# Queries of the last two attentions, projected with tokens on partitions and turned afterwards

## The reference, cut to what matters

```python
# layer 2: 16 heads of 128, 4 key/value heads; rms norm over a head, after a bias
q = (hidden_states @ Wq + bq).reshape(b, s, NH, HD).transpose(0, 2, 1, 3)
q = _rmsnorm(q, qn_w)                     # q * rsqrt(mean(q*q) + eps) * qn_w
scores = jnp.einsum('bhsd,bhed->bhse', q, k) * scale + attention_mask
# layer 3: no bias, but rotary position after the norm; keys from context and stream
q = (draft_hidden @ Wq.T).reshape(bsz, draft_len, H, HD)
q = _rms_norm(q, q_norm_w).transpose(0, 2, 1, 3)
q = _rope(q, draft_position_ids)          # x * cos(emb) + rotate_half(x) * sin(emb)
k = _rope(k, full_position_ids)
```

## Time and profile before

| | us |
|---|---|
| median of 3 runs | 1300.43 (1300.22 to 1301.52) |
| profiled execution | 1304.3 |
| its span in the trace | 1302.5 |

### The profile page before, as it was taken

One profiled execution on the slowest core, in us unless ns is written; L12 is line 12 of the kernel. 1 busy time (PEld: TensorE's weight loads), 2 busy tenths in 40 slices (PEclk: granted clock), 3 DMA queues, 4 the chain that ended last, 5 costly groups with the idle time before them and its releaser, 6 DMA issues.

```text
span 1302.5 us, 22884 instructions
## 1 busy us (share of the span) xinstructions
PE 1147.4 (88%) x8124; PEld 844.3 (65%) x8147; DVE 850.5 (65%) x1920; ACT 621.5 (48%) x1407; POOL 352.9 (27%) x328
## 2 busy tenths in 40 slices
PE   4867869999969999899999988888998999999894
PEld 3554644444455665889988746666657888898753
DVE  7788966888867663455546585333497777775664
ACT  5575435677733343344433422222266766666252
POOL 0040011222121002222222146566422433334032
PEclk8756976999969999899999889899999999999998
DMA  7010034000032235000000262522371000000100
GB/s 257 2 44 1 1 137 203 1 2 2 2 134 91 88 140 174 1 2 1 1 1 1 92 288 84 196 85 86 101 289 66 17 18 17 17 9 9 49 1 33
DMA packets 44571, 89.30 MB, mean 69 GB/s; under 512 B 7280, under 2 KB 30448, under 8 KB 42672
## 3 DMA queue, kind: packets, MB, share of 16 engines
q1 hardware_dynamic: 39184, 73.45, 15.7%
q0 software_dynamic: 5280, 14.42, 3.4%
...
## 4 chain that ended last, share of the span: by engine, by line
PE 65%; DVE 18%; issue 6%; ACT 5%; DMA 2%; POOL 2%; SPq 1%; another core or an unknown queue 1%; DVEq 0%; ACTq 0%; POOLq 0%; PEldq 0%
PE psum L2566 5%; PE psum L2154 4%; PE psum L3183 4%; PE psum L2126 4%; PE psum L3155 3%; PE psum L2586 3%; PE psum L1702 2%; PE psum L1274 2%; PE psum L3056 2%; PE psum L3103 2%; PE psum L2079 2%; PE psum L3125 2%; PE psum L3490 2%; PE psum L2057 2%; PE psum L1720 2%
## 5 line engine op out<-in xcount | busy, mean ns | idle before, releaser
L1469 DVE TENSOR_REDUCE c_max<-psum 128x2 f32<-128x512 f32 x128 | 84.2, 680 | 19.7 <-PE psum L1274 18.2
L1369 ACT ACTIVATE c_probs<-psum 128x512 f32<-128x512 f32 x128 | 75.1, 597 | 35.6 <-PE psum L1285 35.4
L2566 PE MATMUL psum<-m_experts,m_tileT 128*128 x188 | 69.2, 493 | 19.2 <-issue 13.4
L3183 PE MATMUL psum<-a_wo,a_outT 128*128 128x256 f32 x256 | 75.1, 405 | 0.7 <-DVE x_tok L3365 0.7
L2208 ACT ACTIVATE a_probs<-a_probs,a_max 128x64 f32<-128x64 f32 x128 | 42.7, 334 | 44.9 <-DVE a_max L2264 44.9
L3263 ACT ACTIVATE a_probs<-psum,a_max,a_q_rstd 128x128 f32<-128x128 f32 x128 | 56.8, 458 | 11.3 <-DVE a_max L3313 11.2
L2566 PEld LDWEIGHTS psum<-m_experts,m_tileT 128*128 128x128 f32 x188 | 35.8, 199 | 38.6 <-issue 27.9
L2126 PE MATMUL psum<-ctxT_yT_hi,a_wq 128*128 128x128 f32 x256 | 52.9, 290 | 8.2 <-DVE a_qT L2250 7.1
L2875 POOL DMA_INDIRECT m_back<-m_out_tiles,m_rows_of_slots x47 | 46.8, 995 | 46.9 <-DVE m_out_tiles L2809 39.6
L2643 ACT ACTIVATE m_tile_silu<-psum 128x176 f32<-128x176 f32 x47 | 14.9, 318 | 91.0 <-PE psum L2566 56.3
L2250 DVE TENSOR_TENSOR a_qT<-psum,a_columns 128x512 f32<-128x512 f32 x32 | 22.0, 688 | 55.4 <-PE psum L2126 55.4
...
...
## 6 DMA issues: line engine op xcount, KB each, us to landing
...
```

Of the source, the lines that this page charges most:

```text
L1369: e.activation(c1P[:, n % 8, :, :], ps[:, 2 + n % 2, :].rearrange("p (k t) -> p k t", k=2), ACT.Exp, scale=float(1.0 / np.sqrt(np.float32( ...
L1469: e.tensor_reduce(c1M[:, u % 2, j, :], ps[:, c1_score_bank(n), :].rearrange("p (q t) -> p q t", q=2), AX.X, ALU.max).then_inc(c1_mx, 1)
L2566: ins = e.matmul(ps[:, 4 + t % 2, 0:M2_UP], m2xT[:, t % 2, kc, :], m2e[:, bass.ds(own + kc * M2_UP, M2_UP)], start=(kc == 0), stop=(kc == ...
L3183: ins = e.matmul(ps[:, 7, 0:D], a3at[:, i % 2, h, :, :], a3wo[:, h, :], start=(h == 0 and g is None), stop=(h == HQ - 1), skip_group_check ...
```

## The change

- Tokens become the stationary operand and the weights the moving one: two matmuls of 512 columns per group, and the result has tokens on partitions.
- Attention 2: VectorE adds a bias row that is laid out over all partitions (a2_q_bias, 1 MB, loaded over the weights of the keys), writes a2_q_tok, ScalarE squares that, VectorE sums the squares per head (squares_reduced), TensorE turns the group into bank 5 (queries_turned) and ScalarE copies it to a_qT (queriesT). Turned keys move to bank 4, shared with the values.
- Attention 3: ScalarE squares the raw bank; VectorE multiplies by cosine and, half by half, by sine straight from PSUM (queries_read), adds (queries_rotated) and sums the squares (squares_reduced); TensorE turns the group, into the same bank as the raw queries, and ScalarE copies it. The two copies with swapped halves go.
- The square-sum matmuls go. square_sums becomes four small instructions that spread the sums over the partitions that need them, one slot earlier than before.
- In the loops queries_turned comes after heads_out in attention 3 (before keys_turned), and after keys and values in attention 2. In a3_dve queries_read comes before the maxima.
- Queries and keys now use tables of the same form, so MoE 1 makes only one set (two VectorE steps and one ScalarE step fewer, two loads and two stores fewer), and the table of the queries is fetched as the odd 64-element pieces of it, with a small row of norm weights beside. The column tables of attention 3 go.

```diff
-        TRIG_DVE_AT = {9: (0, 0), 10: (0, 1), 11: (1, 0), 12: (1, 1)}
-        TRIG_ACT_AT = {11: 0, 13: 1}
-        TRIG_OUT_AT = {10: 0, 12: 1}
+        TRIG_LOADED = 16 * 2
+        TRIG_DVE_AT = {9: 0, 10: 1}
+        TRIG_ACT_AT = 11
+        TRIG_OUT_AT = 10
...
+        a2bq = nc.alloc_sbuf_tensor_at("a2_q_bias", [P, HQ * HD], F32, offset=ARENA + 4 * KC * HK * HD)
+        m("a2_q_bias_upper", [P, HQ * HD // 2], F32)
...
+            e.wait_ge(*a2_cr.at(NT))
+            e.wait_ge(m1_st, 16 * TILES)
+            e.dma_start(a2bq[:, :], a["a2_bq"].unsqueeze(0).broadcast_to([P, HQ * HD])).then_inc(a2_in.sem, 16)
...
             def queries(g):
                 i, j = g // 4, g % 4
                 if g:
+                    e.wait_ge(*a2_qb.at(g))
+                for kk in range(KC):
+                    ins = e.matmul(ps[:, 6, :], a2tok[kk][:, 1, i * P:(i + 1) * P], a2wq[:, kk, j * 512:(j + 1) * 512], start=(kk == 0), stop=(kk == KC - 1))
+                ins.then_inc(a2_qp.sem, 1)
+
+            def queries_turned(g):
+                e.wait_ge(*a2_qb.at(g + 1))
+                if g:
                     e.wait_ge(*a2_q.at(g))
-                out = ps[:, 6, :].rearrange("p (b h t) -> p b h t", b=2, h=4)
                 for h in range(4):
-                    for kk in range(KC):
-                        ins = e.matmul(out[:, :, h, :], a2wq[:, kk, (4 * j + h) * HD:(4 * j + h + 1) * HD], a2tok[kk][:, 1, i * P:(i + 1) * P],
-                                       start=(kk == 0), stop=(kk == KC - 1))
-                ins.then_inc(a2_qp.sem, 1)
-
-            def out_and_squares(n):
-
-                u, g = a2_group(n, A2_OUT), a2_group(n, 2 - A2_AHEAD)
-                c = (n + 1) % 4
-                if c == 0 and n >= -1:
-                    e.wait_ge(*a2_sr.at(min((n + 5) // 4, NT)))
-                if g is not None:
-                    e.wait_ge(*a2_qf.at(g + 1))
-                if u is not None:
-                    i = u // 4
-                    e.wait_ge(*a2_o.at(2 * i + 1 + c // 2))
-                    if c == 0 and i:
-                        e.wait_ge(*a2_res.at(i))
-                for k in range(4):
-                    if g is not None:
-                        b2, p_ = k // 2, 2 * (g % 4) + k % 2
-                        at_ = D + (p_ // 4) * 8 + (p_ % 4) * 2 + b2
-                        s_ = b2 * 256 + (k % 2) * P
-                        ins = e.matmul(ps[:, 7, at_:at_ + 1], a2qs[:, g % 4, s_:s_ + P], onesf[:, 0:1], start=(c == 0 and k == 0), stop=True,
-                                       skip_group_check=True)
-                        if k == 3:
-                            ins.then_inc(a2_sp.sem, 1)
...
+                    ins = e.transpose(ps[:, 5, h * P:(h + 1) * P], a2qk[:, g % 2, h * HD:(h + 1) * HD], identf[:, :])
+                ins.then_inc(a2_qtp.sem, 1)
+
+            def out_projected(u):
+                i, c = u // 4, u % 4
+                e.wait_ge(*a2_o.at(2 * i + 1 + c // 2))
+                if c == 0 and i:
+                    e.wait_ge(*a2_res.at(i))
+                for h in range(4 * c, 4 * c + 4):
+                    ins = e.matmul(ps[:, 7, 0:D], a2at[:, i % 2, h, :, :], a2wo[h // 8][:, h % 8, :], start=(h == 0), stop=(h == HQ - 1))
+                if c == 3:
+                    ins.then_inc(a2_wp.sem, 1)
...
             def query_squares(g):
-                e.wait_ge(*a2_q.at(g + 1))
-                if g >= 4:
-                    e.wait_ge(*a2_sp.at(g - 3))
-                e.activation(a2qs[:, g % 4, :], a2qT[:, g // 4 % 2, g % 4, :], ACT.Square).then_inc(a2_qf.sem, 1)
+                e.wait_ge(*a2_qb.at(g + 1))
+                if g >= 2:
+                    e.wait_ge(*a2_qd.at(g - 1))
+                e.activation(a2qs[:, g % 2, :], a2qk[:, g % 2, :], ACT.Square).then_inc(a2_qf.sem, 1)
+
+            def queriesT(g):
+                i, j = g // 4, g % 4
+                e.wait_ge(*a2_qtp.at(g + 1))
+                if i >= 2:
+                    e.wait_ge(*a2_s.at(2 * (i - 2) + j // 2 + 1))
+                e.activation(a2qT[:, i % 2, j, :].rearrange("p (b h t) -> p b h t", b=2, h=4), ps[:, 5, :].rearrange("p (h b t) -> p b h t", b=2, h=4),
+                             ACT.Copy).then_inc(a2_q.sem, 1)
...
             def square_sums(i):
-                e.wait_ge(*a2_sp.at(4 * i + 4))
+                e.wait_ge(*a2_qd.at(4 * i + 4))
                 if i >= 2:
                     e.wait_ge(*a2_rq.at(i - 1))
-                e.tensor_scalar(a2qss[:, i % 2, :], ps[:, 7, D:D + 16], HD * 1e-6, None, ALU.add).then_inc(a2_sr.sem, 1)
+                for odd in range(2):
+                    for b2 in range(2):
+                        ins = e.tensor_scalar(a2qss[S * odd:S * odd + S, i % 2, b2:16:2], a2qa[S * b2:S * b2 + S, i % 2, odd:16:2], HD * 1e-6, None, ALU.add)
+                ins.then_inc(a2_sr.sem, 1)
 
             def queries(g):
+                j = g % 4
+                e.wait_ge(*a2_qp.at(g + 1))
+                if g >= 2:
+                    e.wait_ge(*a2_qf.at(g - 1))
+                    e.wait_ge(*a2_qtp.at(g - 1))
+                e.tensor_tensor(a2qk[:, g % 2, :], ps[:, 6, :], a2bq[:, j * 512:(j + 1) * 512], ALU.add).then_inc(a2_qb.sem, 1)
+
+            def squares_reduced(g):
                 i, j = g // 4, g % 4
-                v4 = "p (b h t) -> p b h t"
-                e.wait_ge(*a2_qp.at(g + 1))
+                e.wait_ge(*a2_qf.at(g + 1))
                 if i >= 2:
-                    e.wait_ge(*a2_s.at(2 * (i - 2) + j // 2 + 1))
-                bias = bc(a2c[:, 4 * j:4 * j + 4], 1, 2).unsqueeze(3).broadcast_to([P, 2, 4, S])
-                e.tensor_tensor(a2qT[:, i % 2, j, :].rearrange(v4, b=2, h=4), ps[:, 6, :].rearrange(v4, b=2, h=4), bias, ALU.add).then_inc(a2_q.sem, 1)
+                    e.wait_ge(*a2_sr.at(i - 1))
+                e.tensor_reduce(a2qa[:, i % 2, 4 * j:4 * j + 4], a2qs[:, g % 2, :].rearrange("p (h d) -> p h d", h=4), AX.X, ALU.add).then_inc(a2_qd.sem, 1)
...
-            e.dma_start(a3tr[:, :, :], a["a3_trig"][:, 1, :, :]).then_inc(a3_tq.sem, 16)
+            own = a["a3_trig"].rearrange("p x (i r t) -> p (x i) r t", r=2, t=S)[:, :, 1, :]
+            e.dma_start(a3tr[:, :, :], own).then_inc(a3_tq.sem, 16)
+            e.dma_start(a3qrow[:, :, :], a["a3_q_rows"].unsqueeze(0).broadcast_to([P, 2, HD])).then_inc(a3_tq.sem, 16)
...
-            e.tensor_scalar(a3qcs[:, 0, :], a3tr[:, 1, :], a3c[:, 0:1], None, ALU.mult)
-            dve_step(e, e.tensor_scalar(a3qcs[:, 1, :], a3tr[:, 0, :], a3c[:, 6:7], None, ALU.mult))
+            sin, cos = a3tr[:, 0:NT, :], a3tr[:, NT:2 * NT, :]
+            qc, qs = (a3qcs[:, r, :].rearrange("p (i a t) -> p i a t", i=NT, a=2) for r in range(2))
+            e.tensor_tensor(qc, bc(cos, 2, 2), bc(a3qrow[:, 0, :].rearrange("p (a t) -> p a t", a=2), 1, NT), ALU.mult)
+            e.scalar_tensor_tensor(qs[:, :, 0, :], sin, -1.0, bc(a3qrow[:, 1, 0:64], 1, NT), ALU.mult, ALU.mult)
+            dve_step(e, e.tensor_tensor(qs[:, :, 1, :], sin, bc(a3qrow[:, 1, 64:128], 1, NT), ALU.mult))
...
-                if a3_q_free(g) > 0:
-                    e.wait_ge(*a3_qr.at(a3_q_free(g)))
-                out = ps[:, a3_q_bank(g), :].rearrange("p (b h t) -> p b h t", b=2, h=4)
+                if g == A3_LEAD:
+                    e.wait_ge(*a3_qr.at(g))
+                elif g >= 2:
+                    e.wait_ge(*a3_q.at(g - 1))
+                for kk in range(KC):
+                    ins = e.matmul(ps[:, a3_q_bank(g), :], a3tok[kk][:, 1, i * P:(i + 1) * P], a3wq[:, kk, j * 512:(j + 1) * 512],
+                                   start=(kk == 0), stop=(kk == KC - 1))
+                ins.then_inc(a3_qp.sem, 1)
+
+            def queries_turned(g):
+                e.wait_ge(*a3_rot.at(g + 1))
+                e.wait_ge(*a3_qr.at(g + 1 if g < A3_LEAD - 1 else min(g + 2, A3_U)))
+                if g == A3_U - 1:
+                    e.wait_ge(*a3_q.at(g))
                 for h in range(4):
-                    for kk in range(KC):
-                        ins = e.matmul(out[:, :, h, :], a3wq[:, kk, (4 * j + h) * HD:(4 * j + h + 1) * HD], a3tok[kk][:, 1, i * P:(i + 1) * P],
-                                       start=(kk == 0), stop=(kk == KC - 1))
-                ins.then_inc(a3_qp.sem, 1)
-
...
+                    ins = e.transpose(ps[:, a3_q_bank(g), h * P:(h + 1) * P], a3rot[:, g % 2, h * HD:(h + 1) * HD], identf[:, :])
+                ins.then_inc(a3_qtp.sem, 1)
...
+                if a3_unit(n, 2 - A3_AHEAD) is not None:
+                    queries_turned(n + A3_AHEAD - 2)
...
-            def queries(g):
+            def query_squares(g):
                 e.wait_ge(*a3_qp.at(g + 1))
                 if g >= 4:
-                    e.wait_ge(*a3_sp.at(g - 3))
-                bank = a3_q_bank(g)
-                e.activation(a3qs[:, g % 4, :], ps[:, bank, :], ACT.Square)
-                if g >= 2:
-                    e.wait_ge(*a3_q.at(g - 1))
```

(62 more changed lines are left out.)

192 lines of the change are left out of this document (84 added, 108 removed).

## The result

The changed kernel takes 1333.04 us (median of four runs, 1328.47 to 1336.35) against 1300.33: a ratio of 1.025, interval 1.0218 to 1.0282. It is slower, as forecast, but by 33 us and not by 9.5, and it lies above the range (1328). The profiled execution took 1336.03, its span is 1334.2 against 1302.5.

The account below looks back on a forecast made before the run. In both attention middles only TensorE's work and its waits were taken to count. Attention 2 -7.4, attention 3's middle +7.1 and head +9.6 gave +9.3, rounded to 9.5: median 1310 us, range 1285 to 1328.

Parts of the forecast that it names:

- the price of the four square-sum instructions: Attention 3's middle: in one of two even slots they stand ahead of VectorE's read and take 0.4 to 0.8 us.
- the bound of the middle (+13): Attention 3's middle, forecast +7.1 us: slow bound, if GpSimd slows VectorE's two-input instructions or the small ones are held.
- The clock: Rival, chance 0.20: each late even slot of attention 3 drops the clock, idle past some 1.3 us; +11 to +16, 1325.
- My sign for this rival: Granted clock below 0.95 in attention 3's middle would show that late even slots drop the clock.
- The same-bank wait: Attention 3: turning waits for VectorE's read of the next group in bank 6; TensorE idles 1.1 to 1.6 us, even slots.
- TensorE's saving: TensorE's work per group of queries falls by 0.5 us per slot, nearer 0.4 where no output projection runs.
- P + 2.20: Attention 3's middle: P is a slot's first score matmul; the turning wants its bank released 2.20 us later.
- Attention 2's head: Attention 2, slots 0 to 6: the already late query bias gets 1.3 us worse in two places, +2.6.
- Slots 0 to 6 of attention 3: VectorE's lateness without output projections to cover it: slots 1 to 6 from 38.5 to 44.6 us, low-clock spells +3.
- The leading slots of attention 3: Seven slots start 1 us later for the query tables but wait less for ScalarE: +0.5 us.
- Edits costed at nothing: Query angles leaving MoE 1, the bias row's load, attention 3's sines fetched in pieces: range -0.5 to +2 us.
- The weight loads: Rival, chance 0.02: TensorE's time follows its weight loads; 16 fewer save 3 us per slot, 60 in attention 2, 1235.

Follow-up runs that it names:

- (3): Changed kernel with attention 3's four small square_sums instructions as length-one reductions instead of additions of a constant (constant left out): 1310.0 us, ratio 1.0085.
- (12): Changed kernel with GpSimd's key product in attention 3 covering only 8 of 128 columns per head from the fifth batch on: 1299.17 against 1276.02, ratio 1.0196.
- (8): Changed kernel with 28 extra, unread identity turnings ahead of queries_turned in each attention 3 slot that has the square sums: 1326.14 us, ratio 1.0185.
- (1): Kernel before, with the change made in attention 2 only: 1297.01 us, ratio 0.9978.
- (7): Changed kernel, attention 3: queries turned into bank 2, square_sums behind queries_read, leading slots project group n+7 before turning n+5, turned queries copied after keys: 1298.21 us, ratio 0.9975.
- 10: Changed kernel with attention 3's square_sums as reductions, and squares_reduced there cut to four elements per partition: 1276.53 against 1272.93, ratio 1.0026.
- (9): Changed kernel with attention 3's four square_sums additions done by ScalarE behind its squares instead of by VectorE: 1278.98 against 1272.93, ratio 1.0044.

## Why the prediction was wrong

- **The step that failed** is the price of the four square-sum instructions, "0.4 to 0.8", bounded by the duration of a reciprocal. They take 2.35 us where GpSimd works. The trace of before had a sign of it in reach: two long GpSimd instructions stand together in each even slot (1096.97 and 1097.97), and beside them VectorE's product of two operands in SBUF took 0.97 us (1098.58) and not 0.68 (1105.18, GpSimd idle). The walk through the slot never put GpSimd beside VectorE; I named the case only in the bound of the middle (+13).

```profile
L3325 DVE TENSOR_TENSOR a_q_sin<-a_q_halves_swapped,ctx_tok x18: 681/827/1005, 1043.3 to 1175.0; 128x512 f32<-128x512 f32 x18
```

- **What the hold cost**, with the low clock behind it: attention 3 takes 299.1 us with it and 275.4 without (3), 23.7 less, about the whole miss of 23. That the kernel then takes 1310.0, the very time that I gave, is luck: its leading slots cost 4.3 us and not 0.5, slots 0 to 6 cost 7.3 and not 9.1, the middle 2.0 and not 7.1, and attention 2 gives 3.3 (in the changed kernel) and not 7.4.
- **The clock**, a rival that I gave 0.20, is right in one slot of four, the even one with the square sums: after 3.12 us of idle time it falls every time, after 0.74 or 1.43 us in the middle never, after 2.34 (12) in three of four. I had put its limit near 1.3 us from the earlier trace rows. (The stretch given there for MoE 2 ends before TensorE starts again at 911.24; the clock from 911 to 914 us is 1.00 too, so the reading holds.) My sign for this rival, a mean clock below 0.95 in the middle, did not show (0.95), although the low clock came four times: the sign was set too low. It costs 8 us in the middle (8); without the hold (3) the clock there is 1.00. The rival had the price of a spell right (1.7 us in three of the four; the slot from 1181.94 took 12.37 us and lost 3.0); what made the stall long enough was the hold.
- **The same-bank wait**: right, with its releaser and its slots, and nearly so in size: 1.1 to 1.6 us of idle time were forecast for even slots, 0.74 and, without the hold, 1.43 were measured. The pair of slots with keys and values was forecast at 17.5 and took 17.1; the other was forecast at 14.7 and took 14.4 (7.69 + 6.68) with the hold removed. Without the hold the middle is +2.0 (3), not +7.1: I had 0.36 us too much per pair, nine times, and slot 7 had run at a low clock before (8.24 us, 7.08 in 3).
- **TensorE's saving**: 0.5 us per slot forecast, 0.36 measured in the odd slots, which have no idle time of note (7.04 to 6.68). The 0.13 between is the turning, at P + 2.33 and not 2.20 (1105.59 to 1107.92), the "0.1 to 0.2" of the forecast. In attention 2 it held better: from slot 8 to slot 28 123.8 us became 116.9, of which 2.3 are two new waits at the end (residual, turned keys), so TensorE's work there fell by 9.2 us in 20 slots, 0.46 each. These two waits, which the forecast did not have, are the larger part of what attention 2 missed.
- **Attention 2's head**: +2.6 forecast; leading slots and slots 0 to 7 together took 67.1 before, 70.7 after, 69.0 alone (1). The late bias is where I put it, with idle times of 3.67, 1.66, 3.48 and 5.05 us.
- **Slots 0 to 6 of attention 3**: +9.1 forecast, +13.2 measured, +7.3 with the hold removed (3). Without it the pairs (1,2) and (3,4) take 15.2 and 15.4 us (15.5 and 15.8 forecast), but (5,6) takes 15.8 where I had 13.3.
- **The leading slots of attention 3**: +0.5 forecast, +6.0 measured, +4.3 with the hold removed. Here the walk was too coarse. A turning now stands ahead of the projection, and waits for the rotated sum behind the query tables and the first keys:

```profile
970.06 0.65 PE L3177 MATMUL psum<-ident_f,a_q_rotated 128*128 128x128 f32 x4 [2.98 <-DVE a_q_rotated L3345]
...
989.32 1.11 PE L3177 MATMUL psum<-ident_f,a_q_rotated 128*128 128x128 f32 x4 [4.05 <-DVE a_q_rotated L3345]
```

  A projection before these turnings hardly helped (7), and neither did one reduction less (10: 30.2 us for the leading slots, 29.6 in 3). With the sums on ScalarE (9) they took 29.2. What would bring back the rest was not tried.
- **Edits costed at nothing**: nothing in the runs speaks against it; MoE 1 lies within the scatter above, and the last feed-forward changed by 0.2 us.
- **The weight loads**, a rival that I gave 0.02: the loader was busy 99 us less (844.3 to 745.2), TensorE 12.6 us less, and the kernel is slower. Its time was mis-added, too: 60 us less than 1300 is 1240, not 1235.
